# One dense list of leftover edges in groups of 9 columns, instead of 51 lists in groups of 10

## The reference

```python
# src, dst = both directions of 100000 random pairs, and 6250 self loops; sorted by dst (stable)
# layer 0: h = segment_sum(w[e] * (x @ W)[src[e]], dst), for two weights; attention over three branches
# layer 1: segment_sum, segment_max, count of edge_attr by SRC; then a two-layer MLP
# layer 2: msg[e,k] = gw[e,k] * (x @ g)[src[e], k]; segment_sum by dst; gw from the degrees of src and dst
# layer 3: relu(W1 [x[src], x[dst], edge_attr]) @ W2, segment_sum by dst, then a GRU cell
x = layernorm(x + layer_l(x, ...))   # four times
```

## Time and profile before

| what | before |
|---|---|
| time, median of 3 runs | 7649.85 us (7647.06 to 7652.19) |
| span of the profiled execution, the only time that it has | 9369.1 us |
| mean granted TensorE clock in it | 0.731 of full |
| indirect DMAs of GpSimd: placing, five leftover places | 1632, 510 each |
| placing, 51 blocks | about 3200 us |
| layer0_rest, layer1_scatter, layer 2 edges, layer 3 edges | about 990, 965, 1200, 1890 us |

### The profile page before, as it was taken

One profiled execution on the slowest core, in us unless ns is written; L12 is line 12 of the kernel. 1 busy time (PEld: TensorE's weight loads), 2 busy tenths in 40 slices (PEclk: granted clock), 3 DMA queues, 4 the chain that ended last, 5 costly groups with the idle time before them and its releaser, 6 DMA issues. The chain is left out here.

```text
span 9369.1 us, 138875 instructions
## 1 busy us (share of the span) xinstructions
PE 5537.1 (59%) x49076; PEld 4542.6 (48%) x49077; DVE 5345.0 (57%) x9166; ACT 1663.2 (18%) x3235; POOL 4789.4 (51%) x4394
## 2 busy tenths in 40 slices
PE   2555555555555523233455542899996677777777
PEld 1333333333333322223345441899995566666665
DVE  5555655565556533334344455666665677777773
ACT  0111111111111100002111131000002333333333
POOL 3555555555555454550355551455550577667670
PEclk7666676666666666665666675999996788888885
DMA  3222222221222154441100030111110333333330
GB/s 98 77 82 78 73 75 81 78 78 70 81 78 80 40 92 89 88 88 29 42 20 19 20 109 12 26 26 27 27 27 17 106 100 97 95 93 95 95 92 13
DMA packets 392774, 612.74 MB, mean 65 GB/s; under 512 B 158383, under 2 KB 318995, under 8 KB 377363
## 3 DMA queue, kind: packets, MB, share of 16 engines
q1 hardware_dynamic: 240826, 478.03, 16.7%
q0 software_dynamic: 141056, 124.52, 6.4%
q10 hardware_dynamic: 10454, 4.04, 0.2%
HBM read 531.52 MB, written 216.25 MB: 80 GB/s over the span
## 5 line engine op out<-in xcount | busy, mean ns | idle before, releaser
L321 POOL DMA_INDIRECT pay_d<-row,place x1632 | 1719.7, 1054 | 1524.9 <-DVE place L497 947.9
L415 PE MATMUL win<-onehot,val 128*128 128x128 f32 x4998 | 1045.4, 353 | 672.4 <-issue 455.3
L415 PEld LDWEIGHTS win<-onehot,val 128*128 128x128 f32 x4998 | 872.3, 251 | 926.8 <-issue 644.4
L514 DVE TENSOR_TENSOR onehot<-near_dve,drel 128x896 f32<-128x896 f32 x357 | 389.3, 1091 | 1182.2 <-remote 1057.4
L2113 POOL DMA_INDIRECT m_from_src<-from_src_d,m_row x510 | 684.0, 1341 | 628.5 <-issue 375.4
L1712 PE MATMUL g_win<-g_hot,y_part 128*128 128x128 bf16 x14994 | 880.7, 220 | 145.1 <-DVE g_hot L1761 101.1
L1692 POOL DMA_INDIRECT g_x<-xg_d,g_row x510 | 641.5, 1258 | 625.1 <-PE g_win L1712 411.7
L1712 PEld LDWEIGHTS g_win<-g_hot,y_part 128*128 128x128 bf16 x14994 | 857.3, 99 | 166.8 <-DVE g_hot L1761 102.1
L1091 POOL DMA_INDIRECT sorted_d<-s_row,s_place x510 | 494.1, 969 | 531.0 <-DVE s_place L1207 368.5
L672 POOL DMA_INDIRECT r_x<-in_x,r_row x510 | 485.2, 951 | 500.9 <-DMA r_row<-pay_d 351.2
L2116 POOL DMA_INDIRECT m_from_dst<-from_dst_d,m_row x510 | 631.0, 1237 | 160.0 <-issue 155.7
(11 more groups left out here) (410 smaller groups left out, 11491.4 us busy)
## 6 DMA issues: line engine op xcount, KB each, us to landing
m_hot_t<-drow_d SPq DMA_DIRECT2D x52, 1568.0 KB
scan_d<-in_none SPq DMA_DIRECT2D x51, 1034.2 KB
lo_row<-lo_d SPq DMA_DIRECT2D x51, 1024.0 KB
m_grid<-pay_d SPq DMA_DIRECT2D x52, 882.0 KB
pay_d<-in_fill SPq DMA_DIRECT2D x51, 882.0 KB
grid<-pay_d SPq DMA_DIRECT2D x51, 882.0 KB, 3.8
pay_d<-in_fill SPq DMA_DIRECT2D x51, 720.0 KB
row<-in_pay SPq DMA_DIRECT2D x51, 576.0 KB
```

Of the source, the lines that this page charges most:

```text
L321: pool.indirect_dma_start(a["pay_d"][:, :], bass.IndirectOffsetOnAxis(ap=place[j][:, c:c + 1], axis=0), row[j][:, c, :], None).then_inc(ro ...
L415: mm(win[:, :], val[u % 2][:, s, :], onehot[u % 2][:, s, :], start=(u == 0 and s == 0), stop=(u == NS - 1 and s == SUB - 1))
```

## The change

All leftovers form one list. A running count `ahead` replaces the block's own start, so block b's leftovers follow block b-1's without a gap. SC becomes 9, and group n of the list is rows 1152 n to 1152 n + 1151, no longer tied to block n; the rounds are the list's length over 51 x 1152. A new stage `grouping`, between `placing` and `layer0_rest`, loads the first and the last destination of all 204 possible groups, computes the windows from the widest group (the last group cut at the highest destination, `top`), and broadcasts each group's first destination to all partitions with a matmul (`k.group`). The leftover stages subtract `k.group[n]` instead of `k.base[b]` and add their window at its column. The fill of a leftover region shrinks with SC, from 720 to 648 KB.

```diff
-SC = 10
+SC = 9
 # setup: windows_here, widest, steps, sec_at, win_at are no longer computed here
+                v.tensor_tensor(k.top[:, :], spans[0:1, NBK - 1, 0:1], spans[0:1, NBK - 1, 1:2], ALU.add)
 # placing, places():
-                    v.tensor_copy(k.n_sec[:, at(b)], incl[:, CB - 1:CB])
                     v.tensor_tensor(pos[:, :], incl[:, :], sums[:, CB:2 * CB], ALU.subtract)
                     dve.drain()
-                    v.scalar_tensor_tensor(out=pos[:, :], in0=pos[:, :], scalar=k.sec_at[:, at(b)], in1=sums[:, 0:CB],
+                    v.scalar_tensor_tensor(out=pos[:, :], in0=pos[:, :], scalar=ahead[:, 0:1], in1=sums[:, 0:CB],
                                            op0=ALU.add, op1=ALU.add)
                     dve.drain()
+                    v.tensor_tensor(ahead[:, :], ahead[:, :], incl[:, CB - 1:CB], ALU.add)
 # rounds: leftovers over NBK * SR instead of the fullest block over SR
+def grouping(nc, z, k, a):
+            def _(sp):
+                for e, r in enumerate((0, SR - 1)):
+                    sp.dma_start(ends[:, e, :, :], rows[:, :, r, AT_DST:AT_DST + 2]).then_inc(ends_in, 16)
+            def _(pe):
+                pe.wait_ge(ends_ready, 1)
+                nc.tensor.matmul(first, k.ones[0:1, :], ends_f[:, 0, :], start=True, stop=True).then_inc(first_ready, 1)
+            def _(dve):
+                v.tensor_scalar(steps[:, :], k.iota[0:1, 0:MW], float(WS), None, ALU.mult)
+                dve.wait_ge(ends_in, 32)
+                v.tensor_copy(ends_f[:, :, :], ends[:, :, :, 0].bitcast(i32)).then_inc(ends_ready, 1)
...
+                v.tensor_reduce(widest[:, :], span[:, :], AX, ALU.max)
...
+                v.tensor_reduce(windows[:, :], steps[:, :], AX, ALU.add)
+                dve.drain()
+                v.tensor_copy(k.counts_i[:, 1:2], windows[:, :])
+                v.tensor_scalar(k.win_at[:, :], k.n_at[:, :], windows[:, 0:1], None, ALU.mult)
+                dve.wait_ge(first_ready, 1)
+                v.tensor_copy(k.group[:, :], first)
 # each leftover stage:
-                                 sv[bass.ds(b * NR + r, 1)].rearrange("k p w -> (k p) w")).then_inc(row_in[j], 16)
+                                 sv[at(n)].rearrange("n p w -> (n p) w")).then_inc(row_in[j], 16)
-                    v.tensor_scalar(rel[j][:, :], dst_f[:, :], k.base[:, at(b)], None, ALU.subtract)
+                    v.tensor_scalar(rel[j][:, :], dst_f[:, :], k.group[:, at(n)], None, ALU.subtract)
```

More of the change, by code:

```diff
@@ L243, in placing @@
         incl = sb("incl", [P, CB])
+        ahead = sb("sec_ahead", [P, 1])
         pos = sb("pos", [P, CB])
@@ L441, in _ @@
                 v.memset(k.cnt_sec[:, :], 0.0)
+                v.memset(ahead[:, :], float(z.grid_rows))
                 v.tensor_copy(iota, k.iota[:, :])
@@ L566, in _ @@
                 v.tensor_copy(k.counts_i[:, 0:1], incl[0:1, NR - 1:NR])
+                dve.drain()
+def grouping(nc, z, k, a):
+    G = NR * z.NBK
+    with ExitStack() as ctx:
+        sb, ps, sem = make(nc, ctx)
+        ends = sb("group_ends", [1, 2, G, 2])
+        ends_f = sb("group_ends_f", [1, 2, G])
+        span = sb("group_span", [1, G])
+        widest = sb("widest", [1, 1])
+        steps = sb("steps", [1, MW])
+        windows = sb("windows_here", [1, 1])
+        first = ps("group_first", [P, 512])[:, 0:G]
+        ends_in, ends_ready, first_ready = sem("group_ends_in"), sem("group_ends_ready"), sem("group_first_ready")
+        rows = a["pay_d"][z.grid_rows:z.grid_rows + z.sec_rows, :].rearrange("(a g r) w -> a g r w", a=1, r=SR)
+        with nc.Block() as block:
+            @block.sync
+            def _(sp):
+                for e, r in enumerate((0, SR - 1)):
+                    sp.dma_start(ends[:, e, :, :], rows[:, :, r, AT_DST:AT_DST + 2]).then_inc(ends_in, 16)
+            @block.tensor
+            def _(pe):
+                pe.wait_ge(ends_ready, 1)
+                nc.tensor.matmul(first, k.ones[0:1, :], ends_f[:, 0, :], start=True, stop=True).then_inc(first_ready, 1)
+            @block.vector
+            def _(dve):
+                v = nc.vector
+                v.tensor_scalar(steps[:, :], k.iota[0:1, 0:MW], float(WS), None, ALU.mult)
+                dve.wait_ge(ends_in, 32)
+                v.tensor_copy(ends_f[:, :, :], ends[:, :, :, 0].bitcast(i32)).then_inc(ends_ready, 1)
+                dve.drain()
+                v.scalar_tensor_tensor(out=span[:, :], in0=ends_f[:, 1, :], scalar=k.top[:, 0:1], in1=ends_f[:, 0, :],
+                                       op0=ALU.min, op1=ALU.subtract)
+                dve.drain()
+                v.tensor_reduce(widest[:, :], span[:, :], AX, ALU.max)
+                dve.drain()
+                v.tensor_scalar(widest[:, :], widest[:, :], 0.0, None, ALU.max)
+                dve.drain()
+                v.tensor_scalar(steps[:, :], steps[:, :], widest[:, 0:1], None, ALU.is_le)
+                dve.drain()
+                v.tensor_reduce(windows[:, :], steps[:, :], AX, ALU.add)
+                dve.drain()
+                v.tensor_copy(k.counts_i[:, 1:2], windows[:, :])
+                v.tensor_scalar(k.win_at[:, :], k.n_at[:, :], windows[:, 0:1], None, ALU.mult)
+                dve.wait_ge(first_ready, 1)
+                v.tensor_copy(k.group[:, :], first)
@@ L1062, in _, with load @@
                     clear(i * 2 + 4)
-                def load(at_row, m, j):
+                def load(n, m, j):
                     sp.wait_ge(rows_out[j], m * (SC * 16) + 16)
@@ L2593, in build @@
                     placing(nc, z, k, a)
+                grouping(nc, z, k, a)
                 layer0_rest(nc, z, k, a)
```

50 lines of the change are left out of this document (19 added, 31 removed).

## The result

| | before | after |
|---|---|---|
| median, us | 7648.45 (7642.84 to 7652.19, 4 runs) | 7396.57 (7390.53 to 7401.38, 4 runs) |
| ratio, 95% interval | 1 | 0.9671 [0.9657, 0.9684] |

The kernel after is 252 us (3.3%) faster. The forecast was 7464, 186 us faster, with a range of 7380 to 7550, which holds the time. Its sum is too small by 66 us.

What follows compares the result with a forecast made beforehand. GpSimd's issue was taken to bound layer0_rest and layer1_scatter, TensorE layer 2, and a TensorE, VectorE and ScalarE loop layer 3. Terms -64 - 65 - 28 - 36 + 7 = -186 took 7650 to 7464 us, range 7380 to 7550.

Steps and rivals of the forecast that it cites:

- The gap of 1719 us: Whole kernel before: profiled span 9369.1 us against 7649.85 timed; removing 1733 us of waits left 7636, near the median.
- "remote" waits: Mainly placing and layer 3: VectorE idles on "remote" releases, 1057.4 us in placing; likeliest read as belonging to profiled executions only.
- Layer0_rest and layer1_scatter: GpSimd issues without pause there, so one transfer fewer per group saves 64 us in layer0_rest and 65 in layer1_scatter.
- The first rival: First stages bound by compute loops, not GpSimd's issue: 27 and 36 us saved there, 120 in all, 7530 us; chance 0.15.
- GpSimd's pause of 20 us per triple: Layer0_rest: GpSimd's wait of 20.1 us between runs of 30 gathers, expected still near 20 in the profile after.
- Layer 2: TensorE counts there; the leftover sum falls from 40 to 36 records, saving 28 us; the gathers were hidden.
- Grouping and placing: New grouping stage, in series, costs 7 us (5 to 12); placing taken as 0, the same within 15 us.
- second rival: Waits real in timed runs too, shrinking with the gathers: -81 layer0_rest, -96 layer1_scatter, 260 us in all, 7390; chance 0.12.
- a sign of being wrong: Whole kernel: a timed gain near 120 us (the first rival) or 260 us (the second rival) would show the forecast wrong.
- Layer 3: Loop of TensorE, VectorE and ScalarE sets the pace; less arithmetic saves 36 us (20 to 46), two gathers fewer hide.
- The third rival: GpSimd is layer 3's bound: two gathers fewer per group save 163 us in place of 36, 7337 us; chance 0.04.
- The fourth: A group spans 160 destinations or more, so all leftover stages run a second window: 770 us slower, 8234 us; chance 0.02.

Runs made afterwards that it cites:

- Experiment 9: Kernel after plus a tenth transfer in layer0_rest and layer1_scatter, a tenth column's arithmetic in layer 2, and both in layer 3: 7655.57 us, 1.0013 of before.
- experiment 8: Kernel after with a tenth column of arithmetic in layer0_rest alone and no transfer for it: 7399.25 us, 0.9688 of before.
- after_again: Kernel after, unchanged, measured and profiled again: 7398.65 us, 0.9689 of before.
- before_third: Kernel before, unchanged, profiled a third time, with no "remote" waits: 7649.15 us, profiled span 7647.5 us.
- experiments 6: Kernel after with one more pair of gathers per block in layer 3 alone, into columns nothing reads: 7465.58 us, 0.9777 of before.
- experiment 7: Kernel after with a tenth column of arithmetic in layer 3 alone and no transfer for it: 7397.77 us, 0.9688 of before.
- nine_window_144: Kernel after with windows of 144 destinations in place of 160, still one window: 7348.53 us, 0.9616 of before.

## Why the prediction was right, and where its sum was too small

**The gap of 1719 us.** The prediction placed it in the "remote" waits and took them out, which came within 14 us of the median. The arithmetic held: no execution on chip A has them. The reading that they belong to profiled executions did not: on chip B the timed runs are as long. The first profile's 9369 us is within 1.5% of chip B's 9244 and has the same waits, so I take it to be from such a chip; that is inferred.

**Layer0_rest and layer1_scatter.** Right: -63.8 and -64.7 for -64 and -65, GpSimd issuing with 0.30 us between transfers. Experiment 9 gets both differences back with the transfer alone, and experiment 8 finds nothing in the arithmetic. The first rival is out for chip A. Some of the gain is given back behind layer0_rest: from the start of its last gather to the store of the degrees it is 26.6 us in `after_again` for 18.9 in `before_third`. GpSimd's pause of 20 us per triple, which I expected to see again, is gone (14 waits, 52.1 us with the first one's 48.1).

**Layer 2.** Right: -32.7 for -28; 24 is arithmetic (experiment 9), the rest, at most 9, goes with the transfer, which the prediction called hidden.

**Grouping and placing.** +6.7 for +7. The 2.0 us that the prediction cited stand, in that section, for a transfer that GpSimd issues; SyncE's two loads made VectorE wait 3.38 us here. Placing's transfers keep their 1053 to 1055 ns and 620 us of idle time.

**Luck in the range.** The measured 252 us lie outside the forecast's own band (7425 to 7505, 0.62) and near the 260 us that the prediction named as a sign of being wrong. The range holds them because it was drawn wide enough for the second rival, whose cause is absent on chip A. The sign and three of the four stages were right by their mechanism; the total is in range by that luck.

**Layer 3: the step that failed.** The prediction said that GpSimd's "gathers are held back, not late, and the loop between TensorE, VectorE and ScalarE sets the pace", so that two gathers fewer a group hide, and took 36 us. It had this from 192.0 us of waits on m_pre. On chip A those waits are 8 us in the kernel before, and GpSimd is busy or issuing all the rest of the stage: 1392.3 + 302.9 (issue without the first wait) of 1703.0. The gathers that were said to hide were worth the most: adding the pair back alone costs 67 us, adding the arithmetic back alone nothing (experiments 6 and 7). The third rival, to which I gave 0.04, had the mechanism. Its price of 163 was too high. The difference by terms, from the groups of `before_third` and the kernel after: transfers 1282.2 - 1392.3 = -110.1, issue 274.1 - 302.9 = -28.8, waits for TensorE 34.6 - 7.9 = +26.7, together -112.2. So of a pair's 2.73 + 0.60 us x 51 = 170, the stage kept 112, because the remaining transfers grew (2.79 us a pair for 2.73) and GpSimd now waits for TensorE now and then.

Why these transfers are longer than layer0_rest's 0.95 us shows in order of time, kernel after, GpSimd's instructions and VectorE's larger ones alone:

```profile
6443.69 1.85 DVE L2366 TENSOR_SCALAR m_hot_t<-m_hot_t,iota_p 128x6272 bf16<-128x6272 bf16 x1
6443.89 2.46 POOL L2155 DMA_INDIRECT m_from_dst<-from_dst_d,m_row  x1 [0.30 <-issue]
6445.45 0.62 DVE L2330 TENSOR_TENSOR m_hid<-m_pre,pq 128x448 f32<-128x448 f32 x1
6445.98 0.62 DVE L2336 SCALAR_TENSOR_TENSOR m_left<-m_hid,m_parts 128x448 f32<-128x448 f32 x1
6446.51 0.62 DVE L2342 TENSOR_TENSOR m_parts<-m_left,m_parts 128x448 bf16<-128x448 f32 x1
6446.65 3.37 POOL L2152 DMA_INDIRECT m_from_src<-from_src_d,m_row  x1 [0.31 <-issue]
6447.05 1.09 DVE L2324 TENSOR_TENSOR m_hot<-iota,m_drel 128x896 bf16<-128x896 f32 x1
6448.05 0.62 DVE L2336 SCALAR_TENSOR_TENSOR m_left<-m_hid,m_parts 128x448 f32<-128x448 f32 x1
6448.58 1.35 DVE L2342 TENSOR_TENSOR m_parts<-m_left,m_parts 128x448 bf16<-128x448 f32 x2
6450.33 0.94 POOL L2155 DMA_INDIRECT m_from_dst<-from_dst_d,m_row  x1 [0.30 <-issue]
```

The transfer that starts 0.20 us into VectorE's 1.85 us instruction takes 2.46 and ends 0.81 after it. The one that starts inside m_parts, with four more VectorE instructions behind, takes 3.37. The next starts when no such instruction runs and takes 0.94. Over the whole stage it is what VectorE does at a transfer's start that decides. Of the 918 transfers 286 start while VectorE is idle or in an instruction that reads one tile of SBUF at most (the other input of m_hid, for one, lies in PSUM): each of them takes 0.94 to 0.96 us. The other 632 start inside m_hot_t or inside an instruction that reads two tiles of SBUF (m_hot, m_left, m_parts, m_onehot, the sum of the two tables): 1.60 us in the mean, and 572 of them end about 0.82 (0.78 to 0.85) after that instruction. Layer0_rest is the counterpart: 130 of its transfers start inside the one-hot L768, whose r_near_dve lies in PSUM, and they take 0.951 us, the same as the 195 that start with VectorE idle.

The Trainium skill (page "SBUF — State Buffer", section "Who interferes with whom") says that GpSimd is fully blocked while VectorE holds the port pair that they share; by that the first transfer should end about 0.94 after VectorE's instruction, and the trace agrees with 0.81. For instructions with two inputs in SBUF the same section says that they contend with a GpSimd instruction that reads SBUF, and infers that they do not hold up the making of a transfer. An indirect transfer reads its row numbers from SBUF (m_row), and the trace agrees with the first of the two; which part of the transfer is held up no run separates.

Over the stage this is 1282.2 - 918 x 0.94 = 419 us, and it is how VectorE's columns still cost time in a stage that GpSimd paces: 40 us of transfers between experiments 6 and 9 (1398.6 against 1358.1), 38 between the kernel after and experiment 7. It is also why the remaining transfers grew: in `before_third` 421 of 1020 start unhindered, in the kernel after 286 of 918.

**The other rivals.** The second (waits real) gives 7390, near the measured 7397, and is still not the cause: its terms for the first two stages were -81 and -96. On chip B, where its waits are real, those stages lose 128 and 88 us. The fourth did not come true (116 loads of the scan, one-hots of 128x1440, 102 of them), and its price was some 300 us too low, most of it in layer0_rest, where a second window was put at 2.4 us a group and took 5.5. That run has ten columns, the price was worked out for nine.

**The list itself.** With the tenth column back in its parts the kernel stands at 1.0013 [1.0004, 1.0022] of before, and with ten columns in the list at 1.0046 on chip B. All of the gain is the column that each stage no longer handles. What the list does is to keep the groups full, so that nine columns are enough: one block's own 1,179 leftovers would not fit in 1,152 rows. Its own cost is some 10 us (the interval says 3 to 17), 6.7 of them the grouping stage.

## What to carry to other kernels

When the profiled execution is a fifth longer than the timed ones, first get one that is not: its long waits hide which engine has none left, and here they turned the engine that set layer 3's pace into one that seemed to be held back. Here the engine whose idle time was only its issue gaps set the pace, although VectorE had the larger busy sum (1363 against 1282 us); and a removed instruction there was worth less than its mean, since its neighbours grew. Before pricing a GpSimd transfer, look at what VectorE does when it starts, and where that instruction's inputs lie. Layer0_rest keeps one input of its one-hots in PSUM; the same for layers 2 and 3 was not tried. And where a threshold decides between one pass and two, measure the far side: here a widest group seven destinations over the window costs 14%, and a window cut to one above the widest group is worth another 0.6% or so.

## What was unexpected in the hardware

- The same kernel takes 7632 to 7649 us on one chip and 9244 on another. On the slower one TensorE's matmuls in placing start 0.7 to 1.4 us apart with nothing to wait for (398 us in one group), and the change is worth more there: layer0_rest loses 128 us instead of 64.
- An indirect gather of 128 rows costs GpSimd 0.94 to 0.95 us and 0.30 of issue, however busy VectorE is, unless it starts inside a VectorE instruction with two tiles of input in SBUF or inside m_hot_t; then it takes up to 3.37.
- More work on TensorE did not cost time in layer 3 and came with a higher clock. The stage's windows of `after_again` and of `m_tenth_compute`, in this order (TensorE busy first, granted clock third from the end):

```profile
5595.00:7180.00 1585.00, 1304.54 (x15704) 1114.03 (x15704) 1331.12 (x2001) 657.66 (x1650) 1266.47 (x914) 0.89 0.35 108
```

```profile
5595.00:7180.00 1585.00, 1263.92 (x15909) 1065.70 (x15908) 1357.73 (x2010) 661.07 (x1658) 1304.02 (x913) 0.95 0.35 108
```

With 205 matmuls more in the same window TensorE is busy 41 us less, since a mean of 0.95 has more of the 2.4 GHz level in it than one of 0.89. In `before_third` the mean is 0.93. The waits for TensorE (45 us in `after_again`, 8 in the other two) do not simply follow the clock, though: over the same stage `m_tenth_gathers` has 0.91 with 13 us of them and `nine_window_144` 0.91 with 39. They are short wherever GpSimd has a tenth column's work, in transfers or in their length, and so comes later. What raises the clock was not tested.
